# Twenty VectorE steps over 4352 columns, made in parts of 512

## The chip, the cores and the metric

The kernel runs on one core of a Trainium2 chip. Its engines appear in the profile as PE (TensorE), DVE (VectorE), ACT (ScalarE), POOL (GpSimd) and SP (SyncE). The metric is the device time of one execution in microseconds (us).

## The reference

An image tensor of 2 x 128 channels x 128 x 128 goes through shifted-window attention, then, as 32768 tokens of 128 features, through a mixture of four experts. The gates of the experts come from a graph attention over 524288 random edges and one self loop per token. Cut to what matters here:

```python
h = (x_flat @ W_gat).reshape(M, HEADS, NUM_EXPERTS)          # M = 32768
src = jnp.concatenate([edge_index[0], loops])
dst = jnp.concatenate([edge_index[1], loops])
e = jax.nn.leaky_relu(a_src[src] + a_dst[dst], negative_slope=0.2)
ee = jnp.exp(e - jax.ops.segment_max(e, dst, num_segments=M)[dst])
alpha = ee / (jax.ops.segment_sum(ee, dst, num_segments=M)[dst] + 1e-16)
agg = jax.ops.segment_sum(h[src] * alpha[:, :, None], dst, num_segments=M)
# layernorm, top 2 of 4 experts, softmax gates g, then for each expert:
out = out + g[..., None] * (gelu(x @ W1[ei] + b1[ei]) @ W2[ei] + b2[ei])
```

## The kernel before

**Stages.** Until about 2178 us the kernel does the attention and, beside it on VectorE, sorts the edges by destination. From 2178 to 7895 us it walks through the sorted edges (the gather stage); after that it joins the runs that cross partitions, makes the gates and adds up the experts' outputs.

**The gather stage.** The sorted list has 557056 entries: each partition holds 4096 of the edges (EC) and 256 entries of the sorted tail (TC), 4352 columns in all. The stage works in 68 chunks of 64 columns. In `chunk_pool` GpSimd issues 64 gathers per chunk (L1283); each takes one column of indices from the SBUF tile `idx` and fetches 128 rows of `node_rows` from device memory into `gath`, which has two buffers. `chunk_dve` scans the 64 columns of a chunk: it first evacuates four expert results from PSUM (L1182), makes the masks (L1187 to L1191), waits at L1193 for the chunk's gathers, and goes on from L1195 to the five scans L1223. ScalarE and TensorE do the exponentials and the experts' matmuls of one token block in the same chunk. SP moves data in `chunk_sp`: token loads (L1810), experts' outputs (L1819), result rows (L1822).

**The placement steps.** The end of each destination's run must be known in order later. For that, `place_dve` spreads work over the first 48 chunks, ahead of the chunk's own VectorE work (L1174). `places` is the tile `key_a` read as 4352 int32 columns; `moved` has the same size. Chunks 0 and 1 make the entries: each run end carries the distance that it has to move to the left, all else is zero. Then come 20 steps, one in every second chunk (2, 4, ..., 40): step k picks the entries whose bit k of the distance is set (shift and mask L1115, multiply L1117), and takes them out of `places` (subtract L1119); SP stores `moved` to the DRAM tensor `line` (L1133, L1134) when `moved_made` says so, and in the next chunk loads it back shifted by 2^k entries (L1140, L1142). The next step begins by adding it to `places` (L1110). Chunk 42 makes the last add alone. Each VectorE instruction of a step works on all 4352 columns at once; `own` and `settle` make each wait for the one before. All tiles of a step lie in SBUF.

The exact int32 add shows in the profile as a custom instruction on 8704 halves of 16 bits.

Of the kernel before, what the change touches and what calls it, by code (L numbers as in the profile page):

```python
# [11 lines left out]
ALU = mybir.AluOpType  # L12
# [15 lines left out]
EC = EDGES // P  # L28
TC = M // P
# [131 lines left out]
def program(nc, x, wq_t, bq, wkv_t, bkv, wproj_t, bproj, bias_table, w_gat, att_src, att_dst, b_gat, ln_gamma,  # L161
# [9 lines left out]
    with ExitStack() as ctx:  # L171
        scopes = [ctx]

        def sb(name, shape, dt=F32):
            return scopes[-1].enter_context(nc.sbuf_tensor(name, shape, dt))

        def sem(name):
            return ctx.enter_context(nc.semaphore(name))
# [4 lines left out]
        def con(name):  # L183
            return cst[:, CONST[name][0]:CONST[name][1]]
# [49 lines left out]
        moved_made = sem("moved_made")  # L234
        moved_stored = sem("moved_stored")
        moved_loaded = sem("moved_loaded")
        places_done = sem("places_done")
# [100 lines left out]
        places = keys[0][:, :].bitcast(I32)  # L338
        moved = sb("moved", [P, EC + TC], I32)
# [737 lines left out]
        PLACE_STEPS = 20  # L1077
# [3 lines left out]
        def place_dve(e, c):  # L1081

            def own(ins):
                place_n[0] += 1
                ins.then_inc(place_step, 1)

            def settle():
                e.wait_ge(place_step, place_n[0])

            if c == 0:  # L1090

                e.wait_ge(edges_met, 16 * 3)
                for a, w, o in ((0, EC, 0), (EC + 1, TC, EC)):
                    own(e.tensor_tensor(places[:, o:o + w].bitcast(F32), dst_f[:, a + 1:a + 1 + w],
                                        dst_f[:, a:a + w], ALU.not_equal))
                return
            if c == 1:
                e.wait_ge(ramp_loaded, 16)
                for a, w, o in ((1, EC, 0), (EC + 2, TC, EC)):
                    own(e.tensor_tensor(moved[:, o:o + w].bitcast(F32), moved[:, o:o + w].bitcast(F32),  # L1100
                                        dst_f[:, a:a + w], ALU.subtract))
                settle()
                own(e.tensor_tensor(places, places.bitcast(F32), moved[:, :].bitcast(F32), ALU.mult))
                return
            if c % 2 == 0 and c <= PLACE_LAST:

                k = c // 2 - 1
                if k:
                    e.wait_ge(moved_loaded, 16 * 2 * k)
                    own(e.tensor_tensor(places, places, moved[:, :], ALU.add))  # L1110
                settle()
                if k == PLACE_STEPS:
                    e.sem_inc(places_done, 1)
                    return
                own(e.tensor_scalar(moved[:, :], places, k, 1, ALU.logical_shift_right, ALU.bitwise_and))  # L1115
                settle()
                own(e.tensor_tensor(moved[:, :], moved[:, :], places, ALU.mult))  # L1117
                settle()
                e.tensor_tensor(places, places, moved[:, :], ALU.subtract).then_inc(moved_made, 1)  # L1119
                return  # L1120
            if c == PLACE_LAST + 2:
                e.wait_ge(packed_loaded, 16)
                e.tensor_copy(packed_f[:, :, :], packed_i[:, :, :]).then_inc(packed_ready, 1)
                return
            if c == PLACE_LAST + 4:
                e.wait_ge(packed_turned, 1)
                e.tensor_tensor(end_i[:, :], bank[:, 4, 0:256], con("next_base"), ALU.add).then_inc(ends_done, 1)
# [31 lines left out]
        def chunk_dve(e, c, par, i, at, experts, places_at=None):  # L1159
# [14 lines left out]
            if places_at is not None:  # L1174
                place_dve(e, places_at)
# [741 lines left out]
```

## Time and profile before

| | us |
|---|---|
| median of 3 runs | 8567.37 (8558.14 to 8570.94) |
| the profiled execution | 8560.75 |
| its span, first to last instruction | 8558.6 |
| POOL busy | 4991.7 (58%), 4884 instructions |
| DVE busy | 3777.6 (44%), 3541 instructions |
| PE busy | 2837.0 (33%) |
| ACT busy | 1792.3 (21%) |

A row of the profile names the line, engine, operation, output and input tiles, shapes and count; then busy time and mean duration; then the idle time of the engine just before, with what ended it. "issue" is idle time in which the engine waited for nothing that the profile shows. A row of the timeline has the start and the duration in us, then the instruction. The time of the profiled execution lies 2.15 us above its span.

### The profile page before, as it was taken

To read this page: it belongs to the slowest core of one execution; us is meant where nothing else is said; L and a number is where in the kernel's file an instruction comes from. 1 tells how busy PE (TensorE), PEld (TensorE's weight loads), DVE (VectorE), ACT (ScalarE), POOL (GpSimd) and SP (SyncE) were. 2 spreads that over 40 slices of the span, in tenths; PEclk is the share of its full clock that TensorE was granted. 3 is DMA by queue.
4 is the path that set the end of the run, shared out by engine and by line. 5 is a ranking of instruction groups with operands and counts; after the bars stand their busy time and mean duration, and the time that the engine had idled before them with its cause. 6 is when DMAs were issued, how large, how long until landed. Compare 5 with 4: busy or idle time off the path is not lost.

```text
span 8558.6 us, 47282 instructions
## 1 busy us (share of the span) xinstructions
PE 2837.0 (33%) x14234; PEld 1423.9 (17%) x14234; DVE 3777.6 (44%) x3541; ACT 1792.3 (21%) x2621; POOL 4991.7 (58%) x4884
## 2 busy tenths in 40 slices
PE   2556766666221212112121212121221221200478
PEld 2334444444000000000000000000000000000123
DVE  5998888888332223222322222222121121111699
ACT  1335554443111111111111111111111111110000
POOL 0111112111677777777777777777777777776541
PEclk9778888887665656556565656565665665655555
DMA  1000100000221222222121212221111111111455
GB/s 48 24 25 27 32 30 27 30 27 25 57 70 50 65 54 65 54 60 60 53 66 50 70 50 69 50 70 31 39 39 30 39 39 31 36 26 20 130 186 175
DMA packets 284764, 455.16 MB, mean 53 GB/s; under 512 B 121214, under 2 KB 204382, under 8 KB 262366
## 3 DMA queue, kind: packets, MB, share of 16 engines
q1 hardware_dynamic: 134760, 395.02, 12.6%
q0 software_dynamic: 147648, 56.99, 6.7%
q8 instruction: 108, 1.77, 0.1%
q10 hardware_dynamic: 2208, 1.05, 0.0%
q14 instruction: 40, 0.33, 0.0%
HBM read 231.29 MB, written 221.42 MB: 53 GB/s over the span
## 4 chain that ended last, share of the span: by engine, by line
POOL 52%; issue 18%; DVE 3%; PE 2%; DMA 1%; POOLq 0%; ACT 0%; DVEq 0%
POOL gath L1283 51%; PE bank L1525 1%; DVE yo L1498 1%; POOL got L1564 1%; DVE fin L1503 0%; DMA gate_rows<-gate_dram 0%; DMA gate_dram<-turned_gates 0%; DVE s L1459 0%; DVE sc L1434 0%; POOL first L1715 0%; DVE s L1432 0%; DMA got<-edge_rows,idx_d 0%; DVE sc L1453 0%; DVE sc L1446 0%; DVE sc L1444 0%
## 5 line engine op out<-in xcount | busy, mean ns | idle before, releaser
L1283 POOL DMA_INDIRECT gath<-node_rows,idx x4352 | 4391.3, 1009 | 1326.4 <-issue 1326.4
L1239 PE MATMUL bank<-xm,w_s 128*128 128x512 f32 x1024 | 627.8, 762 | 4242.6 <-ACT scratch_i L1260 4229.7
L1195 DVE TENSOR_TENSOR adst_in<-bank,gath 128x256 f32<-128x256 f32 x68 | 53.5, 786 | 3372.2 <-DMA gath<-node_rows,idx 3372.2
L1239 PEld LDWEIGHTS bank<-xm,w_s 128*128 128x128 f32 x1024 | 227.8, 241 | 4631.6 <-ACT scratch_i L1260 4485.2
L1263 ACT ACTIVATE bank<-diff 128x256 f32<-128x256 f32 x68 | 26.3, 387 | 4227.7 <-DVE diff L1212 4227.7
L1035 POOL TENSOR_TENSOR scratch_i<-xc,dst_f 128x480 f32<-128x480 f32 x64 | 85.7, 1339 | 1303.0 <-ACT dst_f L952 1303.0
L1182 DVE TENSOR_SCALAR scratch_i<-bank,b_s 128x512 f32<-128x512 f32 x256 | 192.1, 751 | 913.4 <-PE bank L1246 521.0
L1246 PE MATMUL bank<-scratch_i,w_s 128*128 128x512 f32 x1024 | 458.2, 600 | 58.2 <-ACT scratch_i L1260 54.7
L1525 PE MATMUL bank<-gate_rows,choose 4*128 4x512 f32 x512 | 447.4, 1064 | 62.2 <-DVE yo L1498 50.7
L1260 ACT ACTIVATE scratch_i<-bank,b_s 128x512 f32<-128x512 f32 x512 | 344.7, 686 | 255.7 <-PE bank L1239 254.9
L1046 POOL TENSOR_TENSOR x<-xc,dst_f 128x512 f32<-128x512 f32 x64 | 126.0, 1989 | 402.3 <-ACT dst_f L952 402.3
L1273 ACT ACTIVATE rows<-sums 128x1280 f32<-128x1280 f32 x68 | 230.5, 3390 | 394.0 <-DVE sums L1223 394.0
L1564 POOL DMA_INDIRECT got<-edge_rows,idx_d x256 | 244.6, 956 | 82.1 <-issue 75.6
L1503 DVE TENSOR_REDUCE fin<-yo 128x512 f32<-128x2560 f32 x64 | 288.0, 4500 | 4.3
L759 PE MATMUL bank<-dst_f,cst 128*128 128x512 f32 x256 | 172.2, 762 | 288.9 <-ACT ot L931 238.6
L419 DVE TENSOR_TENSOR key_b<-key_a 128x1024 f32<-128x1024 f32 (+1 forms) x139 | 257.5, 1852 | 1.8 <-DVEq L597 0.5
L419 DVE TENSOR_TENSOR key_a<-key_b 128x1024 f32<-128x1024 f32 (+1 forms) x144 | 247.0, 1715 | 2.1
L1246 PEld LDWEIGHTS bank<-scratch_i,w_s 128*128 128x128 f32 x1024 | 189.8, 190 | 326.3 <-issue 314.1
L420 DVE TENSOR_TENSOR key_a<-key_b 128x1024 f32<-128x1024 f32 (+1 forms) x144 | 244.1, 1695 | 0.0
L420 DVE TENSOR_TENSOR key_b<-key_a 128x1024 f32<-128x1024 f32 (+1 forms) x139 | 240.2, 1728 | 0.0
L777 PE MATMUL bank<-cst,prob 128*128 128x128 f32 x1024 | 186.9, 327 | 157.8 <-DVE node L672 116.5
L790 PE MATMUL bank<-pt,vb 128*64 128x64 f32 x4096 | 205.7, 245 | 46.4 <-ACT pt L924 44.9
(215 smaller groups left out, 5634.0 us busy)
## 6 DMA issues: line engine op xcount, KB each, us to landing
gath<-node_rows,idx POOLq DMA_INDIRECT x4352
y_dram<-scratch_i SPq DMA_DIRECT2D x64, 1024.0 KB, 4.0
yo<-y_dram SPq DMA_DIRECT2D x64, 1024.0 KB, 5.2
edge_rows<-rows SPq DMA_DIRECT2D x68, 768.0 KB, 3.3
line<-moved SPq DMA_DIRECT2D x21, 2048.0 KB, 7.2
moved<-line SPq DMA_DIRECT2D x20, 2048.0 KB
scratch_i<-in_x SPq DMA_DIRECT2D x64, 256.0 KB, 2.7
x_dram<-x SPq DMA_DIRECT2D x64, 256.0 KB, 2.2
```

Source lines behind the costliest of these rows:

```text
L419: d.step(e.tensor_tensor(small, lower, upper, ALU.min))
L420: d.step(e.tensor_tensor(large, lower, upper, ALU.max))
L790: m = e.matmul(bank[64 * hh:64 * hh + 64, 6 + u % 2, L * w:L * w + L], vb[:, 8 * g + w, hh, v, :], pt[:, w, hh, 64 * v:64 * v + 64], start ...
L1182: e.tensor_scalar(yt[par][:, ex, :], bank[:, 2 + b, :], b2_s[:, ex:ex + 1], None, ALU.add).then_inc(y_evac[b], 1)
L1239: e.matmul(bank[:, k % 2, :], w1_s[:, k // 2, P * (k % 2):P * (k % 2) + P], xm[par][:, :], start=True, stop=True).then_inc(up_full, 1)
L1246: m = e.matmul(bank[:, 2 + b, :], w2_s[:, ex, k, :], hid[:, 2 * ex + k, :], start=k == 0, stop=k == 1)
L1260: e.activation(hid[:, k, :], bank[:, k % 2, :], ACT.Gelu, bias=b1_s[:, k // 2, k % 2:k % 2 + 1]).then_inc(hidden, 1)
L1273: e.activation(rw[:, 0:20], sums[:, :, :, 1:].rearrange("p q h j -> p (q h) j"), ACT.Copy)
L1283: e.indirect_dma_start(gath[par][:, j, :], None, node_rows, bass.IndirectOffsetOnAxis(ap=idx[par][:, j:j + 1].bitcast(U32), axis=0)).then_ ...
L1503: e.tensor_reduce(fin[b][:, :], yo[b][:, :, :].rearrange("c e t -> c t e"), AX, ALU.add).then_inc(fin_ready, 1)
L1525: m = e.matmul(bank[:, 4 * (k % 2) + ex, :], choose[:, ex, :], gate_rows[par][:, 4 * k:4 * k + 4, :].rearrange("e b t -> e (b t)"), start= ...
L1564: e.indirect_dma_start(got[par][:, j, :], None, edge_rows, bass.IndirectOffsetOnAxis(ap=idx_d[par][:, j:j + 1].bitcast(U32), axis=0)).then ...
```

## The change

`place_dve` makes each step in nine parts, eight of 512 columns and one of 256. A part is taken through add, shift and mask, multiply and subtract before the next part begins. Within a part each instruction waits for the one before; the first of the next part does not wait for the last of this one. The signal to SP comes once, after all parts.

```diff
@@ -1107,16 +1107,21 @@
                 k = c // 2 - 1
                 if k:
                     e.wait_ge(moved_loaded, 16 * 2 * k)
-                    own(e.tensor_tensor(places, places, moved[:, :], ALU.add))
-                settle()
-                if k == PLACE_STEPS:
-                    e.sem_inc(places_done, 1)
-                    return
-                own(e.tensor_scalar(moved[:, :], places, k, 1, ALU.logical_shift_right, ALU.bitwise_and))
-                settle()
-                own(e.tensor_tensor(moved[:, :], moved[:, :], places, ALU.mult))
-                settle()
-                e.tensor_tensor(places, places, moved[:, :], ALU.subtract).then_inc(moved_made, 1)
+                for a in range(0, EC + TC, 512):
+                    w = min(512, EC + TC - a)
+                    part, shift = places[:, a:a + w], moved[:, a:a + w]
+                    if k:
+                        own(e.tensor_tensor(part, part, shift, ALU.add))
+                        settle()
+                    if k == PLACE_STEPS:
+                        continue
+                    own(e.tensor_scalar(shift, part, k, 1, ALU.logical_shift_right, ALU.bitwise_and))
+                    settle()
+                    own(e.tensor_tensor(shift, shift, part, ALU.mult))
+                    settle()
+                    own(e.tensor_tensor(part, part, shift, ALU.subtract))
+                settle()
+                e.sem_inc(places_done if k == PLACE_STEPS else moved_made, 1)
                 return
```

## Rows read from the trace of the kernel before

**Rows 1.** The page: chain by line, and the costliest group (busy, mean | idle before).
```profile
POOL gath L1283 51%; PE bank L1525 1%; DVE yo L1498 1%; POOL got L1564 1%; DVE fin L1503 0%; DMA gate_rows<-gate_dram 0%; DMA gate_dram<-turned_gates 0%; DVE s L1459 0%; DVE sc L1434 0%; POOL first L1715 0%; DVE s L1432 0%; DMA got<-edge_rows,idx_d 0%; DVE sc L1453 0%; DVE sc L1446 0%; DVE sc L1444 0%
...
L1283 POOL DMA_INDIRECT gath<-node_rows,idx x4352 | 4391.3, 1009 | 1326.4 <-issue 1326.4
```

**Rows 2.** The gathers' line: duration in ns, least, median, longest; first and last start.
```profile
L1283 POOL DMA_INDIRECT gath<-node_rows,idx x4352: 940/944/6575, 2178.3 to 7894.8; - x198
```

**Rows 3.** Stretches, gathers alone: length, busy (count), TensorE clock, DMA share, GB/s.
```profile
2362.00:5845.00 3483.00, 2698.64 (x2574) 0.60 0.22 59
5845.00:7895.20 2050.20, 1550.37 (x1641) 0.59 0.16 33
```

**Rows 4.** Timeline, GpSimd: beside the first step, the second, and the last add.
```profile
2363.41 2.76 POOL L1283 DMA_INDIRECT gath<-node_rows,idx  x1 [0.30 <-issue]
...
2371.21 4.42 POOL L1283 DMA_INDIRECT gath<-node_rows,idx  x1 [0.30 <-issue]
...
2532.44 6.57 POOL L1283 DMA_INDIRECT gath<-node_rows,idx  x1 [0.30 <-issue]
2539.32 5.12 POOL L1283 DMA_INDIRECT gath<-node_rows,idx  x1 [0.30 <-issue]
2544.75 4.42 POOL L1283 DMA_INDIRECT gath<-node_rows,idx  x1 [0.30 <-issue]
...
5825.45 4.80 POOL L1283 DMA_INDIRECT gath<-node_rows,idx  x1 [0.30 <-issue]
```

**Rows 5.** Timeline, VectorE: the second step, and the chunk's wait for its gathers.
```profile
2531.75 4.69 DVE L1110 CUSTOM_DVE_ANT_0 key_a<-key_a,moved 128x8704 uint16<-128x8704 uint16 x1
2536.47 2.43 DVE L1115 TENSOR_SCALAR moved<-key_a 128x4352 int32<-128x4352 int32 x1
2538.93 4.69 DVE L1117 TENSOR_TENSOR moved<-moved,key_a 128x4352 int32<-128x4352 int32 x1
2543.66 4.69 DVE L1119 TENSOR_TENSOR key_a<-key_a,moved 128x4352 int32<-128x4352 int32 x1
...
2613.09 0.79 DVE L1195 TENSOR_TENSOR adst_in<-bank,gath 128x256 f32<-128x256 f32 x1 [57.62 <-DMA gath<-node_rows,idx]
```

**Rows 6.** Groups of VectorE by shape: short instructions (busy, mean ns | idle before).
```profile
L1446 DVE TENSOR_TENSOR sc<-sc 128x512 f32<-128x512 f32 x8 | 5.5, 692 | 0.3
...
L1187 DVE TENSOR_TENSOR bank<-dst_f 128x256 f32<-128x256 f32 x48 | 20.4, 425 | 0.0
...
L1191 DVE COPY adst_in<-adst 128x4 f32<-128x4 f32 x68 | 11.0, 161 | 0.0
```

**Rows 7.** Timeline: four gathers beside the short two-input instructions L1187 and L1188.
```profile
4461.48 0.48 DVE L1187 TENSOR_TENSOR bank<-dst_f 128x256 f32<-128x256 f32 x1
4461.50 0.94 POOL L1283 DMA_INDIRECT gath<-node_rows,idx  x1 [0.30 <-issue]
...
6331.55 0.42 DVE L1187 TENSOR_TENSOR bank<-dst_f 128x256 f32 x1
6331.58 1.20 POOL L1283 DMA_INDIRECT gath<-node_rows,idx  x1 [0.30 <-issue]
...
6171.34 0.42 DVE L1187 TENSOR_TENSOR bank<-dst_f 128x256 f32<-128x256 f32 x1
6171.58 0.99 POOL L1283 DMA_INDIRECT gath<-node_rows,idx  x1 [0.30 <-issue]
6171.67 0.43 DVE L1188 TENSOR_TENSOR bank<-dst_f 128x256 f32<-128x256 f32 x1
...
3421.07 0.42 DVE L1187 TENSOR_TENSOR bank<-dst_f 128x256 f32<-128x256 f32 x1
3421.36 0.94 POOL L1283 DMA_INDIRECT gath<-node_rows,idx  x1 [0.30 <-issue]
```

**Rows 8.** VectorE's wait for gathers in 2362 to 5845; SP's shifted reload.
```profile
DVE adst_in L1195 <- DMA gath<-node_rows,idx: 2019.9, 40, 57.9
...
2632.60 0.33 SPq L1140 DMA_DIRECT2D moved<-line  x1
```

## Prediction

> **What bounds the kernel now.** I read the page's chain first. Half of it is one line: GpSimd's gather L1283 is 51% of the span [rows 1]. The group row adds the idle time beside it: 4352 gathers, 4391.3 us busy, and 1326.4 us of idle time that ends in "issue" alone. So a gather never waits for data, for a free buffer or for a semaphore. 4391.3 + 1326.4 = 5718 us run from the first gather at 2178.3 to the last at 7894.8 [rows 2]; what shortens a gather shortens the kernel.
>
> The reader should then look at the durations: median 944 ns, longest 6575 ns, mean 1009 [rows 1, 2]. Where are the long ones? The stretches tell: in 2362 to 5845, which holds the placement steps, 2574 gathers are busy for 2698.64 us; in 5845 to 7895, without them, 1641 take 1550.37 us, 0.945 each [rows 3]. 2698.64 - 2574 x 0.9448 = 267 us too much, all of it beside the steps.
>
> One step shows it [rows 4, 5]. VectorE runs add (4.69 us), shift-and (2.43), multiply (4.69) and subtract (4.69), 0.03 us apart, from 2531.75 to 2548.35. In that time GpSimd finishes three gathers, of 6.57, 5.12 and 4.42 us. The second and the third end 0.81 and 0.82 us after the instruction that held them (2543.62 and 2548.35), while the next VectorE instruction already runs; the first, held by the add and then by the shift-and, ends 0.11 after the latter. So a gather is held once near its start by an instruction with both inputs in SBUF, and once near its end by the shift-and; between the two it runs beside VectorE. Cost of a step: (6.57 + 5.12 + 4.42) - 3 x 0.944 = 13.3 us. There are 19 like it (252.5 us), the first step without an add (a gather of 2.76 and two of 4.42 us: 8.8) and the last add alone (4.80 us: 3.9) [rows 4]. Sum 265 us, against 267 from the stretches.
>
> The Trainium skill (SBUF — State Buffer, section "Who interferes with whom") says that a VectorE instruction with two SBUF inputs contends with a GpSimd one that reads SBUF, that a two-port instruction contends with its writes too, and that whichever starts first holds the shared pair for its whole length while the other fully blocks. The rows agree on who contends; on the whole length they differ, as the next part shows. What it would give is a rival below.
>
> **The change part by part.** Removed per full step: 4 VectorE instructions of 4352 columns, 16.5 us. Added: 36, nine parts of add, shift-and, multiply and subtract (eight of 512 columns, one of 256). Durations: a two-input instruction has 0.692 us on 512 columns and 0.425 on 256 [rows 6]. The shift-and on 512 has no row. Between the 2.43 us for 4352 columns and 0.16 us for 4 (L1191, [rows 5, 6]) it is 0.16 + 512 x 2.27/4352 = 0.43; its bounds are 0.29 (2.43 x 512/4352) and 0.69 (no faster than a two-input one). The exact integer add has no short row either; at full length it equals the other two (4.69 [rows 5]), so I take 0.69. Waits between them cost 0.03 us, as now; the next part's add needs no wait, and two such instructions (L1187, L1188) overlap by 0.09 [rows 7]. A part: 3 x 0.69 + 0.43 + 3 x 0.03 - 0.09 = 2.52 us; the train: 8 x 2.52 + 1.70 = 21.9 us against 16.6. VectorE works 5.3 us longer per step.
>
> That costs nothing: behind the steps stand the four evacuations L1182 and then L1195, which waits for the gathers, 57.62 us in this step [rows 5], 2019.9 us in 40 chunks [rows 8]. With 5 us more work and gathers 12 us earlier some 40 us of this cover are left. Without it the price would be 20 x 5.3 = 106 us. On SP the stores L1133 and L1134 wait for the subtract; behind them are queued the token load L1810 and the store L1819, all 5.3 us later. The token load is for the chunk after next, and the shifted reload L1140 goes out at 2632.60, 84 us after the subtract's end [rows 5, 8]. SP's queue loses nothing that anyone waits for. The Trainium skill (VectorE: DVE Perf Modes, "Rules for kernel authors") advises to minimize the count of instructions; by it the sum would carry these 106 us, if VectorE were the bound, which the 57.62 us deny.
>
> What is left of the 265 us? That hangs on when a gather is let in between two short instructions. Rows 7 fix it. A gather that starts 0.02 us after L1187 goes through (0.94) and L1187 is stretched to 0.48; one that starts 0.03 after it is held (1.20). At the other end, a gather that starts with 0.13 us of L1187 left takes 0.94, one with 0.18 left 0.99. So an instruction that lasts d holds the gathers that start between 0.025 us after its own start and 0.135 before its end, and releases them there. The last case was let in even though L1188 had begun. Two dependent instructions 0.03 apart thus leave 0.03 + 0.135 + 0.025 = 0.19 us free, two overlapping ones 0.07. In a part, gather starts are held in 0.025 to 0.56 (add), 0.75 to 1.02 (shift-and), 1.21 to 1.74 (multiply), 1.94 to 2.47 (subtract), then again from 2.54. Gathers come each 1.249 us. From 0.56 the next start is 1.805, free; the next 3.054, that is 0.536 in the following part, held for 0.02. Two gathers (2.498) fit almost exactly into a part (2.52), and the train pulls them into that rhythm: 8 x 0.02 = 0.16 us per step. Before it is reached, the first gather starts 0.69 after the add [rows 4, 5], is free, the second at 1.95 is held for 0.52, and one more may be, for 0.54 (1.20 lies on an edge). To this comes the hold of the shift-and on a gather's end, up to 0.43 once or twice. Together 0.7 to 1.6 us; I take 1.1. If the shift-and took 0.69, a part would last 2.78 and two gathers wait 0.28 in it, 2.4 us per step, within the bounds below.
>
> Bounds for a step: 0 if all slip through, since nothing makes a gather faster than 0.944; and, if a gather gets in only within the bare 0.03 us between instructions, it goes from subtract's end (2.60) to the next multiply's end to the next add's end: three gathers in two parts, 5.04/3 = 1.68 instead of 1.25, 0.43 lost on each of 12: 5.1 us.
>
> Sum: 19 x 1.1 + 1.1 + 0.5 = 22.5 us left of 265, a gain of 242.5. The profiled execution took 8560.75 us (span 8558.6), 6.6 under the median of 8567.4; its forecast is 8318, the median's 8325. Late next is again the gather at its 0.944 + 0.305, as after 5845.
>
> **The rivals.**
> - Narrow gaps. The 5.1 us per step: With 4.7 for the step without an add and 1.2 for the last add, 265 - 19 x 5.1 - 4.7 - 1.2 = 162 gained, 8405. For it: only instructions of 256 columns show the wider gap. Against it: the long ones release with the same 0.81 to 0.82 remainder, which is 0.944 - 0.135.
> - Both block for their whole length: each short instruction waits for the gather in hand, each gather (0.30 later) for the rest of that instruction, 0.69 - 0.30 - 0.135 = 0.25 on 27 of 36: 6.8 us per step, 130 gained, 8437. (That is the rule of the page named above.) Against it: the subtract at 2543.66 started 0.03 after the multiply and lasted 4.69 although a gather ran until 2544.44 [rows 4, 5].
> - Slower: the next short instruction takes its place before the waiting gather. Then one gather hangs through the whole train: it starts 0.69 in and gets on at 21.9 - 0.135, held 21 us instead of 13.3. 19 x 21, 15 for the train without adds and 5.5 for the last adds make 420 against 265: 155 lost, 8722. It decides from the point where a gap is too short for a hand-over. Against it: each of the held gathers got in at a gap of 0.03, and the 0.99 one at an overlap.
> - No change: the gathers' gain is given back, because something else of a chunk is late. For it speaks only that VectorE gets more work; against it the stretch after 5845, where a chunk of 64 runs in 80 us without waiting.
>
> **How the numbers follow.** Forecast (8295 to 8345) 0.76; narrow gaps 0.11; both block 0.05; no change 0.03; slower 0.04; the odd 0.01 lies below 8295. The range takes in the first two: from 8567 - 265 less 10 for the spread of the runs to 8405 plus 7. Measurement tells about 0.2% (17 us) from no change: faster 0.93, same 0.03, slower 0.04.
>
> **What would show it.** L1283: still 4352, mean 953 instead of 1009, idle before it only "issue". No gather in a step over 1.6 us (from 6.57); the gathers of a step mostly 0.94 and 0.96 to 1.0, two per 2.52 us. VectorE: 720 instructions in place of the 80 on L1110, L1115, L1117 and L1119, of 0.69 and 0.43, busy some 105 us more; L1195 still waiting 40 us in each step. Gathers over 4 us only before the first step. The forecast is wrong if steps show gathers of 1.3 to 1.5 us throughout (narrow gaps), VectorE's short instructions stretched to over 1 us (both block), or one gather as long as a train (slower).

## The result, and the profile after

The changed kernel takes 8307.64 us (median of 4 runs, 8296.47 to 8308.23) against 8569.16 for the kernel before beside it: ratio 0.9694, 95% interval 0.9677 to 0.9711. That is 261.5 us less. The profiled execution took 8296.47 us, 264.3 less than the profiled one of before.

The page of the changed kernel, its chain by line and its costliest group. The gather is L1288 here; the step's add, shift-and, multiply and subtract are L1114, L1118, L1120 and L1122; lines behind the steps have numbers five higher than before.

```profile
POOL gath L1288 49%; PE bank L1530 1%; DVE yo L1503 1%; POOL got L1569 1%; DVE fin L1508 0%; DMA gate_rows<-gate_dram 0%; DMA gate_dram<-turned_gates 0%; DVE s L1464 0%; DVE sc L1439 0%; POOL first L1720 0%; DVE s L1437 0%; DMA got<-edge_rows,idx_d 0%; DVE sc L1449 0%; DVE sc L1458 0%; DVE sc L1443 0%
...
L1288 POOL DMA_INDIRECT gath<-node_rows,idx x4352 | 4128.4, 949 | 1326.3 <-issue 1326.3
```

The line of the gathers by duration (least, median, longest), and the two stretches of the gather stage, with and without steps (length, the gathers' busy time and count, clock, DMA share, GB/s):

```profile
L1288 POOL DMA_INDIRECT gath<-node_rows,idx x4352: 940/944/4889, 2178.5 to 7632.0; - x198
```

```profile
2362.00:5650.00 3288.00, 2487.07 (x2629) 0.61 0.24 63
5650.00:7632.90 1982.90, 1499.56 (x1587) 0.59 0.16 34
```

Beside [rows 1 to 3] the count and the idle time are the same, and 4391.3 - 4128.4 = 262.9 us of busy time are gone: all but 1.4 us of the 264.3 between the profiled executions. In the stretch with the steps 2629 gathers take 2487.07 us; at the 0.9449 us of the stretch without, they would take 2484.2. Some 3 us are left of 265.

One step on GpSimd and on VectorE, in the timeline (start, duration; this is the step of [rows 4, 5]):

```profile
2523.30 0.69 DVE L1114 CUSTOM_DVE_ANT_0 key_a<-key_a,moved 128x1024 uint16<-128x1024 uint16 x1
2524.03 0.44 DVE L1118 TENSOR_SCALAR moved<-key_a 128x512 int32<-128x512 int32 x1
2524.51 0.69 DVE L1120 TENSOR_TENSOR moved<-moved,key_a 128x512 int32<-128x512 int32 x1
2525.23 0.75 DVE L1122 TENSOR_TENSOR key_a<-key_a,moved 128x512 int32<-128x512 int32 x1
2525.91 0.68 DVE L1114 CUSTOM_DVE_ANT_0 key_a<-key_a,moved 128x1024 uint16<-128x1024 uint16 x1
...
2530.93 0.68 DVE L1114 CUSTOM_DVE_ANT_0 key_a<-key_a,moved 128x1024 uint16<-128x1024 uint16 x1
...
2533.45 0.68 DVE L1114 CUSTOM_DVE_ANT_0 key_a<-key_a,moved 128x1024 uint16<-128x1024 uint16 x1
```

```profile
2524.01 0.94 POOL L1288 DMA_INDIRECT gath<-node_rows,idx  x1 [0.30 <-issue]
2525.26 0.94 POOL L1288 DMA_INDIRECT gath<-node_rows,idx  x1 [0.30 <-issue]
2526.51 0.94 POOL L1288 DMA_INDIRECT gath<-node_rows,idx  x1 [0.30 <-issue]
...
2532.74 0.94 POOL L1288 DMA_INDIRECT gath<-node_rows,idx  x1 [0.30 <-issue]
2533.99 0.96 POOL L1288 DMA_INDIRECT gath<-node_rows,idx  x1 [0.30 <-issue]
```

The reader should see the rhythm: adds start 2.52 us apart (2530.93, 2533.45), gathers 1.25, so two fall into a part, and what is left of the old holds is, from the fifth part on, a gather of 0.96 in place of 0.94 in most parts, and one of 1.02 in the last. The gather at 2525.26 came 0.03 us after the subtract at 2525.23 and got in; the subtract was stretched to 0.75. VectorE's instructions by shape:

```profile
L1122 DVE TENSOR_TENSOR key_a<-key_a,moved 128x512 int32<-128x512 int32 x160 | 112.0, 700 | 5.4
L1120 DVE TENSOR_TENSOR moved<-moved,key_a 128x512 int32<-128x512 int32 x160 | 111.0, 694 | 5.5
L1114 DVE CUSTOM_DVE_ANT_0 key_a<-key_a,moved 128x1024 uint16<-128x1024 uint16 x160 | 109.4, 684 | 0.9
L1118 DVE TENSOR_SCALAR moved<-key_a 128x512 int32<-128x512 int32 x160 | 69.0, 431 | 5.3
```

### The profile page after: what moved, and what is told of

Read it like the earlier page. It is cut to its first block, busy times and chain, and to the rows that moved or that the text cites. A ratio compares the mean times of both kernels' runs of the same rounds, so it can differ in the third digit from the quotient of the medians.

```text
span 8294.4 us, 47941 instructions
## 1 busy us (share of the span) xinstructions
PE 2878.1 (35%) x14234; PEld 1434.6 (17%) x14234; DVE 3865.5 (47%) x4181; ACT 1791.8 (22%) x2621; POOL 4729.0 (57%) x4884
## 4 chain that ended last, share of the span: by engine, by line
POOL 50%; issue 19%; DVE 3%; PE 1%; DMA 1%; POOLq 0%; ACT 0%; DVEq 0%; SPq 0%
POOL gath L1288 49%; PE bank L1530 1%; DVE yo L1503 1%; POOL got L1569 1%; DVE fin L1508 0%; DMA gate_rows<-gate_dram 0%; DMA gate_dram<-turned_gates 0%; DVE s L1464 0%; DVE sc L1439 0%; POOL first L1720 0%; DVE s L1437 0%; DMA got<-edge_rows,idx_d 0%; DVE sc L1449 0%; DVE sc L1458 0%; DVE sc L1443 0%
## 5 line engine op out<-in xcount | busy, mean ns | idle before, releaser
L1288 POOL DMA_INDIRECT gath<-node_rows,idx x4352 | 4128.4, 949 | 1326.3 <-issue 1326.3
L1200 DVE TENSOR_TENSOR adst_in<-bank,gath 128x256 f32<-128x256 f32 x68 | 53.4, 786 | 2986.3 <-DMA gath<-node_rows,idx 2986.3
L1187 DVE TENSOR_SCALAR scratch_i<-bank,b_s 128x512 f32<-128x512 f32 x256 | 190.4, 750 | 931.9 <-PE bank L1251 535.6
L1251 PE MATMUL bank<-scratch_i,w_s 128*128 128x512 f32 x1024 | 503.5, 645 | 137.3 <-DVE scratch_i L1187 82.6
L1530 PEld LDWEIGHTS bank<-gate_rows,choose 4*128 4x128 f32 x512 | 164.0, 328 | 333.8 <-issue 233.0
```

The costliest lines, as they stand in the source:

```text
L1187: e.tensor_scalar(yt[par][:, ex, :], bank[:, 2 + b, :], b2_s[:, ex:ex + 1], None, ALU.add).then_inc(y_evac[b], 1)
L1251: m = e.matmul(bank[:, 2 + b, :], w2_s[:, ex, k, :], hid[:, 2 * ex + k, :], start=k == 0, stop=k == 1)
L1288: e.indirect_dma_start(gath[par][:, j, :], None, node_rows, bass.IndirectOffsetOnAxis(ap=idx[par][:, j:j + 1].bitcast(U32), axis=0)).then_ ...
L1530: m = e.matmul(bank[:, 4 * (k % 2) + ex, :], choose[:, ex, :], gate_rows[par][:, 4 * k:4 * k + 4, :].rearrange("e b t -> e (b t)"), start= ...
```

## The experiments

The theory: a gather is held near its start by a VectorE instruction with two SBUF inputs, or one of a fast one-input form (the shift-and, a copy), that is running then, until 0.135 us before that instruction's end; a fast one-input form can also hold it near its end. What is lost follows from where the gathers' starts, 1.249 us apart, fall among the instructions; so the time of a step can be walked through (the rhythm). The rivals stand with each run. Each run was compared with the kernel before on the same chip; the changed kernel ran beside it in three of the five sets.

| run | us, median | ratio to before (95%) | under before, us | gathers busy, us |
|---|---|---|---|---|
| changed kernel, second set | 8296.70 | 0.9694 (0.9681 to 0.9708) | 261.5 | 4128.6 |
| 448 columns | 8374.01 | 0.9785 (0.9769 to 0.9801) | 182.7 | 4206.5 |
| 640 columns | 8347.05 | 0.9754 (0.9738 to 0.9770) | 209.7 | 4179.9 |
| 2176 columns | 8495.76 | 0.9928 (0.9911 to 0.9944) | 61.0 | 4327.5 |
| by operation | 8316.31 | 0.9718 (0.9702 to 0.9735) | 240.4 | 4148.4 |
| chunks 0 and 1 too | 8287.40 | 0.9683 (0.9670 to 0.9697) | 270.8 | 4118.4 |
| 32 columns | 8469.41 | 0.9897 (0.9881 to 0.9912) | 88.8 | 4128.0 |
| 16 columns | 10162.73 | 1.1875 (1.1853 to 1.1896) | -1604.5 | 4123.6 |
| four forms, one execution | 8323.67 | | 234.6 | 4156.1 |
| 40 columns | 8297.29 | 0.9693 (0.9677 to 0.9709) | 262.4 | 4129.5 |
| trains shifted | 8304.67 | 0.9704 (0.9686 to 0.9721) | 252.6 | 4134.5 |
| changed kernel, beside the shifted | 8298.04 | 0.9697 (0.9680 to 0.9714) | 259.2 | 4128.4 |

**Other widths** (448 in the diff, then 640 and 2176).

```diff
-                for a in range(0, EC + TC, 512):
-                    w = min(512, EC + TC - a)
+                for a in range(0, EC + TC, 448):
+                    w = min(448, EC + TC - a)
```

> The steps in parts of 448 columns instead of 512 (nine of 448, one of 320). Theory of the rhythm: a two-input instruction of length d holds the gathers that start between 0.027 us after its start and 0.135 before its end; a part then lasts 2.31 us, less than two gathers (2.498), so each gather drifts out of the free places and runs into an instruction again. Walked through by these rules, a full step loses 3.7 us and all steps 75 us, against 3 in the changed kernel: 72 us slower than it, 8380. Rival, the length alone: an instruction can hold a gather for no longer than it lasts, so shorter parts lose no more than 512 does: 8300 to 8312.

> The steps in parts of 640 columns (six of 640, one of 512). Rhythm: a part lasts 3.05 us, a gather finds two free places and is late at one; walked through, a full step loses 2.8 us, all steps 57: 54 us slower than the changed kernel, 8362. Length alone: instructions 19% longer than with 512 columns, so a loss some 20 to 40% above its 3 us: 8308 to 8315.

> The steps in two parts of 2176 columns. Eight instructions of 1.29 to 2.42 us. Rhythm and length alone agree: nearly each instruction holds one gather; walked through, 10.2 us per full step, 204 in all, against 265 for whole instructions: 201 us slower than the changed kernel, 8509. Rival, the number of hand-overs: if the port passed only where VectorE has nothing queued, halving would change nothing against the kernel before: 8560 to 8570.

Measured: 448 columns gain 182.7 us of the changed kernel's 261.5, 79 less (expected 72); 640 columns 52 less (54); 2176 columns 200 less (201). The gathers' busy time says the same: 78, 51 and 199 us above 4128.5. Shorter instructions cost more: the length alone is out, and with 2176 columns a part of the hold is gone, so the gathers do not wait for an idle VectorE. The step with 448 columns, GpSimd in the timeline:

```profile
2692.21 0.94 POOL L1288 DMA_INDIRECT gath<-node_rows,idx  x1 [0.30 <-issue]
2693.45 1.31 POOL L1288 DMA_INDIRECT gath<-node_rows,idx  x1 [0.30 <-issue]
2695.07 1.39 POOL L1288 DMA_INDIRECT gath<-node_rows,idx  x1 [0.30 <-issue]
2696.76 0.94 POOL L1288 DMA_INDIRECT gath<-node_rows,idx  x1 [0.30 <-issue]
2698.01 1.39 POOL L1288 DMA_INDIRECT gath<-node_rows,idx  x1 [0.30 <-issue]
2699.70 1.39 POOL L1288 DMA_INDIRECT gath<-node_rows,idx  x1 [0.30 <-issue]
```

Two of three gathers are held, for 0.37 to 0.45 us: from 2693.45 to 2698.01 three of them take 4.56 us in place of 3.75. The gain of 512 columns is more than that of short instructions: its part happens to be as long as two gathers.

**Order.** All nine adds first, then the nine shift-ands, and so on:

```diff
+                if k:
+                    for at in cuts:
+                        own(e.tensor_tensor(places[:, at], places[:, at], moved[:, at], ALU.add))
+                    settle()
...
```

> Parts of 512 again, but nine adds, then nine shift-and, nine multiplies and nine subtracts, so that within a row of nine no instruction waits and they overlap by 0.08 us. Rhythm: a hand-over also happens at an overlap; instructions start 0.61 us apart, two of them are 1.22, just under a gather's 1.249; walked through, 1.0 to 1.3 us per full step, 22 to 28 us in all: 8327 to 8333. Rival, no hand-over at an overlap: one gather hangs through each row of nine two-input instructions (5.5 us), 12 to 14 us per step: 8550 to 8580.

Measured: 240.4 us under the kernel before, 21 less than the changed kernel; the gathers' busy time is 20 us higher. Expected were 22 to 28 us left in the steps in place of the changed kernel's 3. The first row of nine adds, with two gathers that start in it:

```profile
2524.54 5.37 DVE L1113 CUSTOM_DVE_ANT_0 key_a<-key_a,moved 128x1024 uint16<-128x1024 uint16 x9
...
2525.25 1.41 POOL L1290 DMA_INDIRECT gath<-node_rows,idx  x1 [0.31 <-issue]
2526.96 0.94 POOL L1290 DMA_INDIRECT gath<-node_rows,idx  x1 [0.30 <-issue]
```

Eight adds of 0.69 us and one of 0.46 take 5.37 us together, so they overlap; a gather is held for 0.47 us and not for the row, and the next is free. The hand-over works where VectorE's instructions overlap and leave no idle time at all, and the rival (8550 to 8580) is out.

**What holds a gather.** One unused instruction of 4352 columns in each odd chunk, four forms:

```diff
...
+                if form == 0:
+                    own(e.tensor_tensor(spare[:, :], places, keys[1][:, :].bitcast(I32), ALU.bitwise_and))
+                elif form == 1:
+                    flag = bank[:, 5, 0:1].bitcast(I32).broadcast_to([P, EC + TC])
+                    own(e.tensor_tensor(spare[:, :], places, flag, ALU.bitwise_and))
+                elif form == 2:
+                    own(e.tensor_reduce(spare[:, 0:1].bitcast(F32), dst_f[:, 0:EC + TC], AX, ALU.max))
+                else:
+                    own(e.tensor_copy(spare[:, :].bitcast(F32), dst_f[:, 0:EC + TC]))
```

> The changed kernel with one more VectorE instruction of 4352 columns, whose result is not used, in each odd chunk from 3 to 41; four forms, each five times: (1) an and of two SBUF tiles, (2) an and of an SBUF tile with a PSUM operand, (3) a maximum over one SBUF tile, (4) a copy from SBUF to SBUF. Theory of the holds: form 1 (4.69 us) holds one gather until 0.135 before its end, 4.4 to 5.2 us long; forms 2 and 3, as long but with one SBUF input, hold none, 0.94; form 4 (2.43 us) holds one to its end, 2.3 to 2.8 us. Rival, that any long VectorE instruction holds a gather: forms 2 and 3 show 4.4 to 5.2 us as well. Time: 5 times 3.5 and 5 times 1.5 more than the changed kernel, 25 us; with the rival 60.

In the timeline, each form with the gather that starts in it:

```profile
2926.54 4.69 DVE L1109 TENSOR_TENSOR spare<-key_a,key_b 128x4352 int32<-128x4352 int32 x1
2927.24 4.81 POOL L1302 DMA_INDIRECT gath<-node_rows,idx  x1 [0.30 <-issue]
...
2443.76 4.69 DVE L1112 TENSOR_TENSOR spare<-key_a,bank 128x4352 int32<-128x4352 int32 x1
2444.46 0.94 POOL L1302 DMA_INDIRECT gath<-node_rows,idx  x1 [0.30 <-issue]
...
2603.99 4.68 DVE L1114 TENSOR_REDUCE spare<-dst_f 128x1 f32<-128x4352 f32 x1
2604.68 0.95 POOL L1302 DMA_INDIRECT gath<-node_rows,idx  x1 [0.30 <-issue]
...
2764.43 2.65 DVE L1116 COPY spare<-dst_f 128x4352 f32<-128x4352 f32 x1
2765.13 2.76 POOL L1302 DMA_INDIRECT gath<-node_rows,idx  x1 [0.30 <-issue]
```

Two SBUF inputs hold (4.81), an SBUF and a PSUM input of the same length don't (0.94), a reduction doesn't (0.95), the fast copy does (2.76). All five of each form agree, and the one execution took 8323.67 us, 27 over the changed kernel (25 expected). It is not VectorE's being busy that holds a gather. The Trainium skill (SBUF — State Buffer, "Who interferes with whom") says of these forms which contend with a GpSimd instruction that reads SBUF (two SBUF inputs, and a copy in a two-port mode) and which don't, and the trace agrees in all four; an older probe that the section mentions, in which `tensor_tensor` did not stall DMA, is not what these gathers show (4.81).

The PSUM operand of the second form is one column repeated. That PSUM, and not the repetition, sets the gather free shows in the changed kernel at L1200 (L1195 before), whose PSUM operand is a full tile of 256 columns:

```profile
2591.51 0.78 DVE L1200 TENSOR_TENSOR adst_in<-bank,gath 128x256 f32<-128x256 f32 x1 [36.86 <-DMA gath<-node_rows,idx]
2591.57 0.94 POOL L1288 DMA_INDIRECT gath<-node_rows,idx  x1 [0.30 <-issue]
```

The copy holds a gather at its start, just as two inputs do: the gather ends 0.81 us after the copy (2767.89 against 2767.08), so it got in 0.13 before the copy's end. The copy itself took 2.65 us where 2.43 was expected, and so did the shift-and of the first step in the kernel before; why was not tested.

**The phase.** One short VectorE instruction with a PSUM operand ahead of each train:

```diff
...
+                flag = bank[:, 5, 0:1].bitcast(I32).broadcast_to([P, 256])
+                own(e.tensor_tensor(spare[:, 0:256], dst_f[:, 0:256].bitcast(I32), flag, ALU.bitwise_and))
+                settle()
```

> The changed kernel with one VectorE instruction of 256 columns (one SBUF, one PSUM operand, 0.43 us, result not used) before each step, so that the trains begin 0.46 us later against the gathers. Theory of the rhythm: the first gather now starts 0.24 us after the add, inside the add's hold, and is held to 0.56 (1.2 to 1.3 us long); after that two gathers fit into a part again. 0.5 to 0.65 us per step instead of 0.13, in all 8 to 11 us more than the changed kernel. Rival, that with parts of 512 columns no phase matters: no gather of a step over 1.03 us in the steps with adds, time as the changed kernel within 3 us.

> The changed kernel on the chip of this call, as the base for the shifted one: 0.969 of the kernel before in all theories, 0.12 to 0.14 us per step with adds.

The start of a shifted train, in the timeline:

```profile
2525.21 0.69 DVE L1118 CUSTOM_DVE_ANT_0 key_a<-key_a,moved 128x1024 uint16<-128x1024 uint16 x1
2525.45 1.27 POOL L1292 DMA_INDIRECT gath<-node_rows,idx  x1 [0.30 <-issue]
2527.02 0.94 POOL L1292 DMA_INDIRECT gath<-node_rows,idx  x1 [0.30 <-issue]
```

The gather starts 0.24 us into the add and lasts 1.27, as expected; the next is free. Time: 6.6 us over the changed kernel beside it, a little less than the 8 to 11 expected; the gathers are busy 6.1 us longer. So the phase at which a train begins decides the few tenths of a us that a step of 512 columns still costs.

**The last long instructions.** Chunks 0 and 1 hold three gathers in the changed kernel:

```diff
-                for a, w, o in ((0, EC, 0), (EC + 1, TC, EC)):
+                for a, w, o in ((*((a, 512, a) for a in range(0, EC, 512)), (EC + 1, TC, EC))):
...
```

The part left out does the same to chunk 1, where the subtract and the multiply now go part by part.

> The changed kernel, and also chunks 0 and 1 (the compare L1094, the subtract L1100 and the multiply L1103, 4096 to 4352 columns each) in parts of 512. In the changed kernel their three long instructions still hold a gather each, for 3.94, 3.60 and 3.81 us. Theory of the holds: these 11.3 us go but for 1 to 2: 9 to 11 us under the changed kernel, longest gather of the stage under 2 us. Rival, that the start of the stage is hidden behind other waits: no difference over 3 us.

> The changed kernel itself, on the chip of this call, as the base for the others. All theories: the ratio seen before, 0.969, so some 262 us under the kernel before; gathers busy 4128 us.

Measured beside each other: 8287.40 (8285.74 to 8289.44) against 8296.70 (8292.66 to 8299.43), 9.3 us less; the longest gather fell from 4894 to 1207 ns. This version beats both kernels.

**The cover.** Narrower parts lengthen VectorE's train, with next to no hold of the gathers:

> The steps in 136 parts of 32 columns: 544 instructions of 0.18 to 0.19 us per step, a train of 106 us instead of 22. Theory of the cover: VectorE falls 84 us behind in a step's chunk, takes the gathers of that chunk late by some 45 us and catches up in the next chunk; the two gather buffers give 80 us, so GpSimd never waits: within 5 us of the changed kernel, gathers lose 4 us in the steps. Rival, that a step has only the 57.6 us of VectorE's own wait as cover: 20 times (84 - 45) = 780 us slower.

> The steps in 272 parts of 16 columns, 1088 instructions of 0.17 us, a train of 195 us: longer than the 160 us that a pair of chunks takes on GpSimd. Theory of the cover: VectorE becomes the bound of the stage in the steps; a pair takes the train and VectorE's other work of two chunks, some 20 us each, 235 to 245 us: 20 times 75 to 85 us, 9800 to 10000, and the gathers show idle time that ends in VectorE (the buffer's release at L1217 of before). Rival, that VectorE's work never reaches GpSimd: as the changed kernel.

> The steps in 109 parts of 40 columns. Theory of the cover, mended by the runs with 32 and 16: VectorE bounds a pair of chunks when its train and 57 us of other work and waits exceed the pair's 160 us of gathers, so from a train of 102 us on. With 32 columns a part took 0.83 us; with 40 it takes 0.86, the train 93 to 95 us: no gather waits for VectorE, and the holds cost nearly nothing: 0.969 to 0.970 of the kernel before, as the changed kernel. Rival, that the loss grows in proportion to the train from the changed kernel's 22 us on (173 us at 113 us of train, 1.9 us per us): 135 to 140 us slower than the changed kernel, 0.985 to 0.986.

The waits of GpSimd, in the stretch of the steps, with 32 columns and then with 16 (waited for: us in total, times, longest):

```profile
POOL gath L1288 <- issue: 790.8, 2595, 0.3
POOL gath L1288 <- DVE terms L1222: 177.4, 18, 10.8
```

```profile
POOL gath L1288 <- DVE terms L1222: 1877.4, 20, 98.3
POOL gath L1288 <- issue: 815.8, 2677, 0.3
```

With 32 columns the expectation failed, on both sides: 173 us slower than the changed kernel, not 0 to 5 and not 780. No gather is held in the steps any more, but 18 times GpSimd waits, for up to 10.8 us, for L1222, which gives the gather buffer back. From the seventh step on the trains start 170.7 us apart, of which the train takes 113.1 (106 were expected); the other 57.6 are VectorE's work and waits in two chunks. What was left out is a wait in the odd chunk, where nothing hides the experts' chain:

```profile
2657.01 2.44 DVE L1228 TENSOR_TENSOR_SCAN sums<-bank,terms 128x260 f32<-128x260 f32 x4
2659.56 3.39 ACT L1278 ACTIVATE rows<-sums 128x1280 f32<-128x1280 f32 x1 [5.77 <-DVE sums L1228]
2673.74 7.13 PE L1251 MATMUL bank<-scratch_i,w_s 128*128 128x512 f32 x16 [0.86 <-ACT scratch_i L1265]
2675.82 0.75 DVE L1187 TENSOR_SCALAR scratch_i<-bank,b_s 128x512 f32<-128x512 f32 x1 [16.37 <-issue]
```

VectorE stands idle for 16.37 us. The row names nothing that it waits for ("issue"); the order of the rows says that it is the first expert: ScalarE turns to the experts after VectorE's last scan, TensorE makes the expert's output from 2673.74 on, and L1187 evacuates it. With that, VectorE bounds a pair by the sum from a train of 160 - 57.6 = 102 us on. The 16-column run fits: a train of 199.9 us, 256 us per pair, waits of GpSimd of 1877.4 us in all, 1866 us over the changed kernel (1500 to 1700 expected, from a train of 195). The run with 40 columns was made to test it: train 90.8 us, no gather waits for VectorE, 262.4 us under the kernel before, the same as the changed kernel. So the runs put the limit between 90.8 and 113.1 us.

## Why the prediction was right

- The bound, right: the idle time of the gathers stayed at 1326.3 us of "issue", and what was taken from gathers came off the time one for one (262.9 of busy time, 261.5 in the medians). Nothing else became late.
- The 265 us, right: 3 us of them are left in the steps.
- The train, right: 21.87 us against 21.9 forecast, 0.69 and 0.43 us per instruction; the exact add at 0.684 included. The terms of a part as written (3 x 0.69 + 0.43 + 3 x 0.03 - 0.09) add up to 2.50, not 2.52; the chip's part is 2.52, with gaps of 0.03 to 0.04 and an overlap of 0.08, so the figure on which the rhythm of two gathers (2.498) hangs came out right in part by luck. VectorE is busy 87.9 us longer, not 105: the prediction took the train's length for busy time, but the gaps between dependent instructions (17.1 us in the rows by shape above) lengthen the train and are idle. Its wait for the gathers in this step fell from 57.62 to 36.86 us (40 forecast), in the row of L1200 above.

- The residue, too large: 1.1 us per step were taken, 0.14 measured (2.9 us over 20 steps and the last add), 22.5 against 3 in all. This is what separates 8325 from 8308. The term that failed is the hold of the second gather, and with it the possible hold of a third (0.54) and of a gather's end by the shift-and (0.43), neither of which happened in the step shown. The prediction put the second gather's start at 1.95 and the subtract's hold from 1.94 on, 0.52 us lost. On the chip that gather starts 0.03 us after the subtract, at the very edge, and goes in ([rows 7] show a gather at 0.03 that was held, so the edge lies at about 0.03, not at 0.025); the subtract pays with 0.06. That a few hundredths of a us decided it is luck. The walk into a rhythm, two gathers per part and 0.02 lost in each, is what the trace shows from the fifth part on. The shifted run shows the price where the first gather falls inside a hold: 0.3 us more per step.
- The cover for VectorE was understood too loosely: 57.62 us of wait in one chunk was named, while a train of 90.8 us costs nothing and one of 113.1 does. The limit is that of a pair of chunks, 102 us by the sum, because the step's delay can be made up in the next chunk.
- Of the rivals, "narrow gaps" (5.1 us per step) and "both block for their whole length" are out: a step loses 0.14 us and not 5.1 or 6.8, and of the short instructions only single ones are stretched, those with two inputs by 0.06 us, the first shift-and of the first step from 0.43 to 0.65. "Slower" is out too; a gather gets in at each hand-over, even at an overlap.

## What to carry to other kernels

Where GpSimd issues indirect gathers one after the other, look at the longest of them and at what VectorE does then; an instruction with two SBUF inputs, or a fast one-input form, holds a gather that starts in it until about 0.13 us before its own end. A PSUM operand takes the hold away; shorter instructions shorten it. Cutting is not steadily better the finer it is: walk the gathers' period through the parts, and choose a width at which they fall into step (512 here, with 448 and 640 losing 79 and 52 us). Parts of 40 columns, with instructions of 0.20 us, did as well without that, since little is left of an instruction in which a gather can be held; but their train is close to the limit of the cover. The extra fixed cost of the pieces is free as long as VectorE's work of a whole round stays under the gathers' time; find that limit, with the waits in it.

## What the runs showed of the hardware

The hold ends some 0.13 us before the end that the trace gives for VectorE's instruction, and it begins about 0.03 after its start, so that two instructions 0.03 us apart leave 0.19 us in which gathers get in; walks by such numbers (0.135 and 0.025 to 0.027) came within 8 us of the measured differences in the seven runs that they were made for, from 7 to 200 us. The hold works the other way for a moment only: a VectorE instruction with two SBUF inputs that finds a gather at that point is stretched by 0.06 us, not by the gather's 0.94. And shorter instructions can cost more than longer ones: in place of 0.14 us per step, the parts of 448 columns lose some 4 (78 us in 20 steps).
